# Waiting once for the largest count: VectorE's gathering of maxima in a two-layer transformer kernel

## The reference: what is computed

```python
x = x + L0_attn(layernorm(x))   # one head, key and value width 64, causal softmax, biases
x = x + L0_ffn(layernorm(x))    # one product, activations and weights rounded to 8-bit floats
x = x + L1_attn(layernorm(x))   # 16 heads of width 16, rotary embedding (rope) of Q and K, causal
x = x + L1_ffn(layernorm(x))    # sigmoid(xr Wr) * (relu(xk Wk)^2 Wv), xr and xk mix x with the row before
```

## Time and profile before

| what | value |
|---|---|
| median of 3 runs | 2520.64 us |
| the runs | 2513.99, 2520.64, 2524.67 us |
| span of the profiled execution | 2514.1 us (no other time of that execution is given) |
| TensorE granted clock, mean | 0.981 of full speed |
| nmax steps: the reduction L1558 | 128 instructions, 39.0 us idle before them |

### The profile page before, as it was taken

The page is one execution under the profiler, slowest core; times in us unless marked ns, Lnnn a source line. Parts: engine busy times, 40 slices in busy tenths (PEclk is TensorE's granted clock), DMA queues, the critical chain, the costliest instruction groups (busy, mean ns, idle before and its releaser), DMA issues.

```text
span 2514.1 us, 52353 instructions
## 1 busy us (share of the span) xinstructions
PE 2320.8 (92%) x19371; PEld 1053.0 (42%) x19371; DVE 1985.3 (79%) x4326; ACT 1512.4 (60%) x2753; POOL 525.7 (21%) x526
## 2 busy tenths in 40 slices
PE   8889899999999899998999999999999999999998
PEld 4544333333434335353444534344344434332345
DVE  5778689887787887879787787997788688899932
ACT  2234456575655666676675666657566577677762
POOL 5453210302215012120403303031121400000011
PEclk9899999999999999999999999999999999999999
DMA  2322220120211312021121302112021121110111
GB/s 56 83 72 73 76 58 25 38 59 18 83 34 35 82 43 73 15 79 29 42 65 37 91 19 76 40 35 78 12 76 35 42 70 45 31 42 27 28 37 36
DMA packets 185896, 125.41 MB, mean 50 GB/s; under 512 B 84912, under 2 KB 185392, under 8 KB 185648
## 3 DMA queue, kind: packets, MB, share of 16 engines
q1 hardware_dynamic: 184880, 121.16, 17.4%
q10 hardware_dynamic: 768, 0.92, 0.1%
HBM read 62.20 MB, written 59.24 MB: 48 GB/s over the span
## 4 chain that ended last, share of the span: by engine, by line
PE 55%; DVE 29%; ACT 6%; issue 4%; DMA 2%; SPq 2%; DVEq 1%; POOL 1%; POOLq 0%; ACTq 0%
DVE mx L1543 20%; PE psum L1867 12%; PE psum L1845 6%; PE psum L1812 6%; PE psum L1778 4%; ACT probs L1303 4%; PE psum L1742 3%; PE psum L1887 2%; PE psum L1713 2%; PE psum L1898 2%; PE psum L1651 2%; PE psum L1918 2%; PE psum L1799 2%; PE psum L1906 2%; DVE stats L1402 1%
## 5 line engine op out<-in xcount | busy, mean ns | idle before, releaser
L1303 ACT ACTIVATE probs<-psum 128x512 f32<-128x512 f32 x2176 | 1139.4, 607 | 465.8 <-PE psum L1845 310.2
L1543 DVE TENSOR_REDUCE mx<-psum 128x1 f32<-128x512 f32 (+2 forms) x2304 | 1283.4, 620 | 140.9 <-PE psum L1812 99.5
L1867 PE MATMUL psum<-probs,vs 128*17 128x512 f32 (+3 forms) x5120 | 590.7, 543 | 0.7 <-ACT probs L1303 0.3
L1812 PE MATMUL psum<-kst,qst 48*128 48x512 f16 (+3 forms) x2560 | 439.6, 354 | 71.0 <-DVE mx L1543 37.7
L1845 PE MATMUL psum<-qst,kst 50*128 50x512 f16 (+3 forms) x2560 | 428.7, 353 | 55.7 <-DVE mx L1543 19.5
L1812 PEld LDWEIGHTS psum<-kst,qst 48*128 48x128 f16 x2560 | 134.0, 94 | 397.5 <-DVE mx L1543 154.5
L1845 PEld LDWEIGHTS psum<-qst,kst 50*128 50x128 f16 x2560 | 128.2, 94 | 360.1 <-ACT probs L1303 131.4
L1867 PEld LDWEIGHTS psum<-probs,vs 128*17 128x17 f32 x5120 | 93.1, 96 | 155.5 <-issue 127.6
L1088 POOL TENSOR_SCALAR vare<-mv 128x4 f32<-128x4 f32 x64 | 15.5, 241 | 595.5 <-DVE mv L1405 595.5
L1819 PE MATMUL psum<-maskq,identh 64*128 64x128 bf16 (+1 forms) x2048 | 131.1, 205 | 0.0
L1117 POOL TENSOR_TENSOR sums<-probs 128x512 f32<-128x512 f32 x12 | 15.3, 1272 | 494.3 <-ACT probs L1257 494.3
(11 more groups left out here) (173 smaller groups left out, 2876.2 us busy)
## 6 DMA issues: line engine op xcount, KB each, us to landing
qk_dram<-parts SPq DMA_DIRECT2D x168, 128.0 KB
qst<-qk_dram SPq DMA_DIRECT2D x128, 96.0 KB, 2.3
kst<-qk_dram SPq DMA_DIRECT2D x128, 96.0 KB, 2.3
v_dram<-vst SPq DMA_DIRECT2D x64, 136.0 KB, 4.0
vs<-v_dram SPq DMA_DIRECT2D x64, 136.0 KB, 2.1
xs<-x_in SPq DMA_DIRECT2D x16, 512.0 KB, 3.5
x_dram<-xs SPq DMA_DIRECT2D x16, 512.0 KB, 2.9
att_dram<-ast SPq DMA_DIRECT2D x64, 128.0 KB, 2.0
```

Source lines behind the costliest of these rows:

```text
L1303: act.activation(dst, src, ACT.Exp, scale=DK1 ** -0.5 / LIFT ** 2).then_inc(S["exp"], 1)
L1543: ins = dve.tensor_reduce(mx1[:, n % 2, 2 * g + odd, tile % TPC, c:c + 1], bank(src, at, at + cols), AX.X, ALU.max)
L1812: ins = pe.matmul(two[odd][:, at:at + cols], qst[rows, qslot, pair, P * (tile % TPC):P * (tile % TPC + 1)], kst[rows, kslot, pair, 0:cols] ...
L1867: ins = pe.matmul(bank(7, off, CH, rows=VW, row=32 * h), vtile[:, h, :], probs[:, HG * (step_no(b, hg, k) % PSTEPS) + h, at:at + CH - off] ...
```

## The change

A new method `jobs` takes a list of items, finds the largest of their counts and waits for that alone. The three places on VectorE that waited for each item of a list in turn now call it: nmax0 for its "max0 d" steps, rope for the four RT transposes of the chunk that used the buffer before, and nmax for its "max d" steps.

```diff
@@ class Waits
+    def jobs(self, kind, items):
+
+        counts = [COUNT[kind, item] for item in items]
+        if counts:
+            self.wait_ge(kind, max(counts))
@@ VectorE, nmax0
-                    for i in range(TPC * q, TPC * (q + 1), 2):
-                        for c in range(q + 1):
-                            wt.job("max0 d", (b, i, c))
+                    wt.jobs("max0 d", [(b, i, c) for i in range(TPC * q, TPC * (q + 1), 2) for c in range(q + 1)])
@@ VectorE, rope
-                    for bl in range(4):
-                        wt.job("RT", old and (*old, bl))
+                    wt.jobs("RT", [(*old, bl) for bl in range(4)] if old else [])
@@ VectorE, nmax
-                    for unit in max_units(b, hg, q):
-                        for odd in range(2):
-                            wt.job("max d", (*unit, odd))
+                    wt.jobs("max d", [(*unit, odd) for unit in max_units(b, hg, q) for odd in range(2)])
```

## The result

| | before | after |
|---|---|---|
| median | 2518.86 us (4 runs, 2513.99 to 2524.67) | 2479.62 us (4 runs, 2475.36 to 2481.80) |
| span of the profiled execution | 2514.1 us | 2473.9 us |
| TensorE idle in it (span less busy) | 193.3 us | 169.5 us |
| TensorE busy in it | 2320.8 us | 2304.4 us |
| VectorE idle before the nmax reduction | 39.0 us | 0.6 us |

The ratio is 0.9846, 95% interval 0.9826 to 0.9867: 39 us faster. The sign was right and the gain, 39.2 us, was 1.7 times the forecast one. Of the 17.4 us between forecast and time, 1.8 come from the median of the kernel before, which is 2518.86 us with the fourth run and was 2520.64 in the forecast; 15.7 us are gain that the sum did not have.

A forecast was written before the change was run, and what follows sets the result against it. TensorE, busy 2320.8 of 2514.1 us, was taken as the bound, so only its idle time could be won: 17.2 + 6.3 = 23.5 us, from 2520.64 to 2497 us, with a range of 2481 to 2513.

The forecast's parts named there:

- the sum: TensorE waits expected to go: 17.2 us at its transpose of the maxima, 6.3 us for PSUM banks, together 23.5 us.
- Where the idle time comes from: VectorE before the nmax reduction: 39.0 us idle from queued waits, 0.10 us per two-count entry, about 1 us covered.
- (a) nmax: One wait in each of nmax's 64 blocks: 1024 queue entries fewer, VectorE wins 35.4 us of idle time.
- (b): One wait in nmax0's 16 blocks: taken as 0, bounds 0 and 6.4 us.
- (c): One wait in rope, 14 steps affected: taken as 0, bounds 0 and 1.4 us.
- How much reaches the end: VectorE's 35.4 us counts only where TensorE stood still for it: 23.5 us of span.
- rival 1: The whole chain gets shorter: all 35.4 us of VectorE's idle time reach the end, 2485 us; chance 0.22.
- Rival 2: TensorE takes back half of the 17.2 us at its transpose in later waits: 8.6 us won, 2512 us; chance 0.20.
- Rival 3: The waits cost nothing: one wait takes as long as 29, the time stays at 2521 us; chance 0.06.
- Rival 4: Slower through GpSimd's port: earlier gatherings meet its long additions, 27 more hits give 2537 us; chance 0.04.
- The range: 8 in 10 for the median time: 2481 to 2513 us, low end from all 35.4 us reaching the end.
- The signs to look for: Changed profile: wait entries 1615 to about 560, idle before nmax some 4 us, transpose wait 3 to 5 us.

The follow-up runs named there:

- e4: The changed kernel, but nmax waits for every second of its counts, the last included; 2484.45 us, ratio to before 0.9856.
- e5: The kernel before, with each of nmax's waits emitted twice; 2636.38 us, ratio to before 1.0474.
- e6: The changed kernel, where each "max d" step also waits for its own step eight places back, long done; 2480.30 us, ratio to before 0.9850.
- e2: The changed kernel with nmax's single waits put back, so only nmax0 and rope wait once; 2510.82 us, ratio to before 0.9972.
- e1: The kernel before with the new method used only in nmax; 2476.70 us, ratio to before 0.9819.
- e7: The changed kernel, with one wait also in TensorE's values steps and rope transposes and SyncE's loads; 2480.26 us, ratio to before 0.9855.
- e3: The kernel before, all waits kept, with five useless TensorE products before the wait for nmax in 8 of 64 blocks; 2511.02 us, ratio 0.9970.
- e9: The kernel before with nmax's waits emitted twice, plus 5 to 18 useless TensorE products before the wait in 22 blocks; 2611.04 us, ratio 1.0381.
- e8: The changed kernel without the 311 TensorE products whose results nobody uses; 2508.54 us, ratio to before 0.9967.

## Why the prediction was wrong

- *Where the idle time comes from*: right. 0.10 us an entry, two counts to an entry, a cover of about 1 us. e4, e5 and e6 bear it out, with fewer entries, with more, and with as many beside running work. The idle time in e5 was some 20 us less than this reckoning gives (133.8 against 155).
- *(a) nmax*: VectorE won 39.0 - 0.6 = 38.4 us where 35.4 were named. At q = 0 I took the 0.9 us for the time that the last reduction needs to end; with one wait only 0.2 us is left there, and with three entries (e4) it is 0.8, so it was the entries. A small miss.
- *(b) and (c)*: 0 in the rest, as taken (e2: 2466.2 against 2465.9). What e2 still shows is clock.
- *How much reaches the end*: the sum of 23.5 us was made of TensorE's idle time, and TensorE's idle time fell by 23.8 us in the profiled executions. Over the runs the rest fell by 28.5 us; in e1, e6 and e7, which also wait once in nmax, it fell by 24.8, 25.4 and 24.0. So this part of the forecast was right, within a few microseconds; where the change's own 5 us above 23.5 come from is not shown.
- **The step that failed** is the one that this sum rests on: "that is all that any change to waits can win, as long as its own work stays the same". The number of products stayed the same, but the time that they take did not: TensorE's busy time fell by 16.4 us, 23.8 + 16.4 = 40.2 us of span. The missing term is TensorE's clock, which the sum had put at nothing without a reason. This stall made TensorE pause for up to 2 us, behind some of the pauses the clock stood at half speed, and the clock part fell by 10.6 us over the runs (by 11.1 to 14.9 in e1, e6 and e7). That is two thirds or more of the 15.7 us. e3 and e9 show the pause as the cause: with VectorE's stall in place, filling TensorE's pause took the half clock away behind it and brought time back. How much of 10.6 us is this stall's doing is known less well, since e2 moved the clock part by 5.4 us without touching a stall. The mean granted clock of 0.981 stood in the table before; the granted clock in the half-microseconds behind the gap at 572.39 would have shown the 0.50, and I did not price it.
- *The rivals*: rival 1 had nearly the right time (2485 us) for a reason that the trace refutes in part: TensorE's idle time ended at 169.5 us, the 170 of the forecast, and not under 160. Rival 2, that TensorE takes it back, did not happen. Rival 3 is refuted by e5 alone. Rival 4's hits stayed as they were, two at TensorE's transpose.
- *The range* reached below the forecast only to the chain's 35.4 us. That was no lower bound: where a stall also slows the engine that waits for it, it can cost more than its own length, as e5 shows with 120 us for 94.8.
- *The signs to look for*: entries 459, and not 560, since nmax kept none of its own (1088 went where 1024 were named); idle time 0.6 in place of 4 us; the wait at the transpose 2.7 us (3 to 5 named).

## What to carry to other kernels

Waits that ask for ascending counts of one semaphore say no more than the last of them; where more stand in a row than the running instruction covers, wait once for the largest. To price a stall, look at TensorE's granted clock just behind it as well as at the idle time: the products that follow a pause may run at half speed, and that is a term of its own. Split each run into (1 - clock) x span and the rest before comparing kernels that are less than a per cent apart.

## What the runs showed of the hardware that was not expected

- The granted clock of one and the same program differed from run to run, 0.975 to 0.985, and with it the time, 2531.74 to 2508.05 us; nearly all of the spread of the kernel before goes along with it (correlation 0.94).
- 311 products without use, 82 us of TensorE's busy time, make the changed kernel 29 us faster (e8), since without them 51 us more go to the half clock.
- A run of uncovered waits that made TensorE pause for up to 5.2 us cost as much again in clock as in pause: 60.4 and 59.8 us (e5).
- The half clock came behind pauses as short as 0.90 us (at 400.12, with more pauses around it), and not behind every pause of that length: behind seven of twelve at the transpose in the kernel before. It also came behind a row of waits for PSUM banks of 0.5 to 0.8 us each, from 872.81 to 876.33 us, and there it stood for 10.2 us.
